# One step of a GRU with its feed-forward layer: the first product before the bias, and the token squares after n's input products

## The reference, cut to what matters

```python
def cell(h, x):                       # 32 steps, one after the other
    gi = x @ W_ih + b_ih              # 3 gates r, z, n of 256 columns each
    gh = h @ W_hh + b_hh
    r = sigmoid(i_r + h_r); z = sigmoid(i_z + h_z)
    n = tanh(i_n + r * h_n)
    h_new = (1.0 - z) * n + z * h
...
gu = h_all @ ternary_quant(w_gate_up).T      # for every token (b, t)
gate, up = split(gu)
hid = silu(gate) * up
hn = hid * rsqrt(mean(hid * hid) + eps)      # the mean square of a token
out = x + hn @ ternary_quant(w_proj).T
```

## Time and profile before

| | us |
|---|---|
| median of 3 runs | 346.22 (346.09 to 346.31) |
| the profiled execution, its own time | 346.3 |
| its span, first to last instruction | 344.5 |
| TensorE busy | 339.4 (99%) |
| DVE busy | 233.6 (68%) |
| ACT busy | 222.8 (65%) |
| POOL busy | 184.0 (53%) |

### The profile page before, as it was taken

How to read it: one execution, slowest core, us unless ns; L and a number is a source line. 1 busy time by engine, 2 the same in 40 slices (tenths; PEclk the granted TensorE clock), 3 DMA queues, 4 the chain that set the end, 5 groups by cost and what they waited for, 6 DMA issues and landing times.

```text
span 344.5 us, 5631 instructions
## 1 busy us (share of the span) xinstructions
PE 339.4 (99%) x2059; PEld 295.2 (86%) x2059; DVE 233.6 (68%) x462; ACT 222.8 (65%) x438; POOL 184.0 (53%) x156
## 2 busy tenths in 40 slices
PE   8999999999999999999999999999999999999996
PEld 4889988788988889888888889888888888888895
DVE  7578788899677565755667554875558555664866
ACT  5768888886756757555766656566564655756662
POOL 2315571465825446255454446444472554799694
PEclk9999999999999999999999999999999999999999
DMA  7994000045001000140001000010000100010101
GB/s 240 319 410 192 3 0 2 0 148 220 1 2 62 2 0 0 44 142 2 0 0 63 0 2 0 2 63 0 2 0 2 60 1 2 0 64 1 57 6 61
DMA packets 7891, 18.72 MB, mean 54 GB/s; under 512 B 564, under 2 KB 4788, under 8 KB 7352
## 3 DMA queue, kind: packets, MB, share of 16 engines
q1 hardware_dynamic: 7176, 17.97, 13.9%
q10 hardware_dynamic: 688, 0.39, 0.4%
HBM read 14.17 MB, written 4.19 MB: 53 GB/s over the span
## 4 chain that ended last, share of the span: by engine, by line
PE 94%; DVE 3%; ACT 1%; issue 1%; DVEq 0%
PE ps_ffn L1105 30%; PE ps_out L1143 16%; PE ps_rz L1017 7%; PE ps_rz L1022 7%; PE ps_rz L1018 7%; PE ps_n L1017 3%; PE ps_n L1022 3%; PE ps_n L1018 3%; PE ps_rz L1105 2%; PE ps_ffn L1270 2%; PE ps_t L1098 1%; PE ps_ffn L1017 1%; PE ps_ffn L1022 1%; PE ps_ffn L1018 1%; PE ps_n L1055 1%
## 5 line engine op out<-in xcount | busy, mean ns | idle before, releaser
L354 POOL TENSOR_TENSOR hid_lo<-work,hid_hi 128x512 fp32r<-128x512 f32 x62 | 81.7, 1317 | 103.6 <-ACT hid_hi L452 99.6
L1105 PE MATMUL ps_ffn<-st_hi,wguT 128*128 128x512 f32 x236 | 93.7, 397 | 0.3 <-DVE work L737 0.3
L1105 PE MATMUL ps_ffn<-st_lo,wguT 128*128 128x512 f32 x236 | 92.7, 393 | 0.0
L361 POOL TENSOR_TENSOR sq_sum<-sq_sum,work 128x512 f32<-128x512 f32 x55 | 73.2, 1331 | 1.8 <-ACT work L466 0.6
L737 DVE TENSOR_TENSOR work<-work,ps_ffn 128x512 f32<-128x512 f32 x55 | 37.6, 683 | 31.5 <-ACT work L448 31.5
L452 ACT CAST hid_hi<-work 128x512 fp32r<-128x512 f32 x63 | 38.8, 616 | 23.0 <-DVE work L747 23.0
L1105 PEld LDWEIGHTS ps_ffn<-st_hi,wguT 128*128 128x128 f32 x236 | 44.4, 188 | 8.3 <-DVE work L737 0.9
L1105 PEld LDWEIGHTS ps_ffn<-st_lo,wguT 128*128 128x128 f32 x236 | 44.5, 189 | 7.3
L747 DVE TENSOR_TENSOR work<-work,ps_ffn 128x512 f32<-128x512 f32 x63 | 43.2, 686 | 4.7 <-PE ps_ffn L1105 2.8
L1143 PEld LDWEIGHTS ps_out<-wpT,hid_hi 128*128 128x128 f32 x240 | 35.8, 189 | 3.7
L1143 PE MATMUL ps_out<-wpT,hid_lo 128*128 128x256 f32 x240 | 38.8, 284 | 0.0
(11 more groups left out here) (226 smaller groups left out, 716.0 us busy)
## 6 DMA issues: line engine op xcount, KB each, us to landing
out_dram<-o_st SPq DMA_DIRECT2D x7, 512.0 KB, 2.6
xT_all<-in_x_dram SPq DMA_DIRECT2D x1, 3072.0 KB, 17.6
x_ring<-in_x_dram SPq DMA_DIRECT2D x1, 3072.0 KB, 11.5
x_ring<-in_L_ffn_w_gate_up_dram SPq DMA_DIRECT2D x4, 512.0 KB, 8.9
x_ring<-in_L_ffn_w_proj_dram SPq DMA_DIRECT2D x2, 512.0 KB, 11.6
x_ring<-in_x_dram SPq DMA_DIRECT2D x1, 1024.0 KB, 5.4
work<-in_L_cond_W_ih_dram SPq DMA_DIRECT2D x3, 256.0 KB, 4.4
work<-in_L_cond_W_hh_dram SPq DMA_DIRECT2D x3, 256.0 KB, 4.6
```

The lines of the kernel that those rows point to most:

```text
L354: nc.gpsimd.tensor_tensor(hid_lo[:, j % RING], hid[:, j % 2], f32(hid_hi[:, j % RING]), ALU.subtract).then_inc(hid_lo_ok, 1)
L361: nc.gpsimd.tensor_tensor(sq_sum[:], sq_sum[:], hid_sq[:, j % 2], ALU.add).then_inc(sq_added, 1)
L1105: mm = pe.matmul(bank, w, group_state(part, G, k), start=(k == 0 and i == 0), stop=(k == KD - 1 and i == 1))
```

## The change

Three edits.

1. In `PE_BEFORE[0]` the last two items change places: the six matmuls of `n` come first, then the 12 of `S`, and right behind them `transpose_state`.
2. The zeros of `q_keep` are written in two halves. TensorE waits for the first half alone and runs 11 warm-up matmuls where it ran 12; these read only the first half. DVE waits for both halves before it copies them.
3. In step 0 `first_input(0)` runs before the wait for `b_split_ok`, and its first matmul opens the bank. The bias matmul follows it and adds.

```diff
-PE_BEFORE = [["C6", "G0", "in", "C7", "U0", "G1", "S", "n"], ["G2", "U2", "in", "D0"],
+PE_BEFORE = [["C6", "G0", "in", "C7", "U0", "G1", "n", "S"], ["G2", "U2", "in", "D0"],
...
-            nc.vector.memset(q_keep[:], 0.0).then_inc(warm_ok, 1)
-            dve.wait_ge(warm_ok, 1)
+            nc.vector.memset(q_keep[:, 0], 0.0).then_inc(warm_ok, 1)
+            nc.vector.memset(q_keep[:, 1], 0.0).then_inc(warm_ok, 1)
+            dve.wait_ge(warm_ok, 2)
...
-                        pe.matmul(dst, part[:, 0, k, :], wi_hi[:, k, cols], start=False, stop=False,
-                                  skip_group_check=True)
+                        pe.matmul(dst, part[:, 0, k, :], wi_hi[:, k, cols],
+                                  start=i == 0 and k == 0 and part is xT_hi, stop=False, skip_group_check=True)
...
             pe.wait_ge(warm_ok, 1)
-            busy(12)
+            busy(11)
             pe.wait_ge(consts, 5)
+            first_input(0, ps_rz[:, 0:D])
             pe.wait_ge(b_split_ok, 1)
-            seed_rz(0)
-            first_input(0, ps_rz[:, 0:D])
+            bias_rows(ps_rz[:], RZ, False)
             first_state(0, ps_rz[:, 0:D], r_sum)
```

## The result

| | before | changed |
|---|---|---|
| median, first comparison | 346.26 us (4 runs) | 348.91 us (348.40 to 349.32, 4 runs) |
| ratio, 95% interval | | 1.0071 (1.0059 to 1.0083) |
| median, second comparison | 346.41 (16 runs) | 348.31 (348.27 to 348.62, 5 runs) |
| its ratio | | 1.0055 (1.0042 to 1.0069) |
| profiled execution, its span | 346.3, 344.5 | 348.55, 346.6 |

The change makes the kernel slower, by 2.65 us in the first comparison and by 1.90 in the second. The direction and the place are as forecast, the span is 0.35 above it (346.25 forecast, 346.6 measured). The first median lies 0.1 us above the top of my range and 0.9 above the forecast; the second, 348.31, is 0.3 above the forecast.

The account below looks back on a forecast made before the run. TensorE's own order was taken to bound the kernel. From 346.3 us, five holds of 0.40 added 2.0 and the start took off 0.25, giving 348.05, or about 348.0 against the median; range 347.3 to 348.8.

Parts of the forecast that it names:

- What bounds the kernel: Whole span: TensorE's own order sets the end, so any pause in its issue adds to the time in full.
- The hold: Transposes at t = 12 to 28 wait for DVE's mean: 0.40 us at each of five steps, +2.0 us.
- for a load that can partly overlap: Transposes' weight load after DVE's mean: a little allowed for overlap, in taking 0.40 us between 0.31 and 0.42.
- The rivals of no hold and of 0.6: At the transposes: hold next to nothing, 345.5 or 346.0, chance 0.05; or 0.6 a place, 349.0, chance 0.08.
- No engine falls further behind: Behind the held transposes: ACT and DVE slide along, POOL's 4.55 us idle absorbs its 0.7 us later start.
- The start, -0.25: Step 0's sum: shorter warm-up and first input ahead of the bias gain 0.25 us, range 0 to 0.35.
- warm-up holds step 0, by up to 0.6 us: Kernel start: warm-up issues until 6.57 us, though `wi_hi` is ready at 5.98 and `b_split` at 6.19.
- the start gives nothing: Rival at step 0: DVE's `wh_lo` and the hand-overs hold it where it was; 348.2 us, chance 0.12.
- behind this sum all slides; no DMA is waited for: After step 0's sum: everything moves with it; no DMA waits after 5.36 us on ACT, 3.07 on DVE.
- The second half of the zeros costs nothing: DVE at the start: 0.75 us idle before it needs the biases at 3.07, so `b_split` stays in place.
- The clock comes late: Rival at the start: clock rises at 11.4 us instead of 6.9, losing 2.25 us; 350.2 us, chance 0.05.

Follow-up runs that it names:

- the order alone: Kernel before with only the token squares S moved behind n's products, start unchanged: 348.27 us median, ratio 1.0052 to the kernel before.
- the halves: Kernel before with only the zeros written in halves and 11 warm-up matmuls, bias still first: 346.64 us median, ratio 1.0006.

## Why the prediction was right, and where it was not

**What bounds the kernel.** Right. TensorE's pauses were never given back: 5 x 0.43 of hold made 2.1 of span, and 0.20 to 0.21 a place made 1.04.

**The hold.** Right in place and mechanism, with 0.40 taken and 0.43 measured. The working had given 0.42. Term by term: the hand-over from the squares to the mean took 0.05 (0.04 forecast), the mean 0.16, and from its end to the transposes 0.15 (0.16). The room that I left "for a load that can partly overlap" was not there. The rivals of no hold and of 0.6 fall.

**No engine falls further behind.** Right: ACT stays 0.44 behind the transposes, POOL idles on.

**The start, -0.25.** Wrong: the fastest runs and the profiles show a gain of 0 within 0.1. (The ratios alone, 1.0000 and 0.9999 with 0.3 us to either side, would still allow it.) Two steps of the prediction failed.

The first is "warm-up holds step 0, by up to 0.6 us", counted against a product at 8.14. In the profile of before the bias matmul starts at 6.34; with the same warm-up in the profile of the order alone, TensorE waits for `b_split` and starts it at 6.36:

```profile
6.34 0.77 PE L1028 MATMUL ps_rz<-b_split,neg_ones 128*128 128x512 f32 x1
```
```profile
1.45 4.40 PE L1270 MATMUL ps_ffn<-q_keep 128*128 128x512 bf16 x12 [1.45 <-DVE q_keep L845]
...
6.36 0.47 PE L1028 MATMUL ps_rz<-b_split,neg_ones 128*128 128x512 f32 x1 [0.51 <-DVE b_split L858]
...
7.08 0.67 DVE L869 TENSOR_TENSOR wh_lo<-work,wh_hi 128x512 fp32r<-128x512 f32 x1
...
7.85 0.46 PE L1303 MATMUL ps_rz<-wh_lo,st_hi 128*128 128x256 f32 x2
```

Five kernels with 12 warm-up matmuls and the bias first wait for `b_split` like this and start the bias at 6.31 to 6.37. So the biases, ready at 6.19, held step 0, and the warm-up hid behind them. What was late before is the clock: the 12 warm-up matmuls took 5.30 us there, 4.40 here, and the bias matmul 0.61 to the next start against 0.31 (the prediction read it as 0.38 from 6.57). With the clock up in time and the weights on time, the last product of gate r starts at 7.80 to 7.85 with no edit of the start, and at 7.87 to 7.90 with the input first. DVE ended `wh_lo` here at 7.75, as I had it (7.74), and it caps this product in both orders. So 8.14 was no fair base, and the case "the start gives nothing" (348.2) was the right one.

The second is "behind this sum all slides; no DMA is waited for". In the result's profile gate z's W_hh was waited for, by 0.22. This one moves from execution to execution: with the input first it is there in two profiles and under 0.05 in four, and with the bias first it is there in two profiles whose loads nobody had moved. That W_hh lands at 9.4 "whatever TensorE does", as I expected after the result, is therefore wrong: ACT starts on it at 9.11 in the second profile of the changed kernel.

The Trainium skill (TensorE: Matmul & The Clock Gate, Part 1) says that the point of the rise differs from run to run; the profiles here agree, with 4.06 to 5.30 us for 12 warm-up matmuls.

**The second half of the zeros costs nothing.** Right where I looked, at the biases; what I did not price is that the queue is one instruction longer. That costs TensorE about 0.2 in the order of before and nothing in the changed one.

**The clock comes late**, at 11.4 us. Did not happen in any of thirteen profiles. With the start edits pairs of 256-column matmuls follow each other at 0.24, the spacing of 2.4 GHz, from 8 us at the latest, not from 11.

**The level.** The first four runs had a median 0.6 above the second five. The profile of the first set (348.55) explains 2.1 of its difference; two other runs of that set had spans of 347.3 and 347.4 and left no profile. That they had a late landing like the one at 6.25 us in the profile of the halves (ACT's first weight, span 0.8 longer) fits, but was not shown.

## What to carry to other kernels

When a small product is moved towards the instruction that waits for its reader, count the round trip: here it was 0.52 us from the start of the last small matmul through VectorE's result to the next TensorE write, and what is short of it comes back once per iteration, in full, on a TensorE that never idles. Before an edit that makes an engine earlier, compare the landing times of its loads with the new schedule and not with the list of waits: the 0.22 that ACT waited for W_hh has no row in its list here, and only the chain names it. And take the start of a kernel from several profiles: clock and landings alone moved it by 0.8 us here, more than the edits of it could.

## What the runs showed of the hardware

One instruction more at the head of DVE's queue, even a 2-column memset, delays a product 213 us later by 0.34 us, at the same step in every kernel that has one, and in none without. With the order of before, two DMA packets of the queue of kind "instruction" fall between 215.3 and 217 us with and without it, behind the start of the product; that the added instruction moves the point where the queue is refilled was my theory, and no run shows it. What is shown is the place, the size and that it follows the count of instructions.

A matmul of one column passes its sum on fast: 0.16 us, and DVE starts 0.05 later; the way back from DVE's end into TensorE's weight load is 0.11 here (141.22 to 141.33), where two waits stand in front of it, and was 0.05 with one. That the second wait makes the difference was not tested.
